# Four layers over eight batches: the quantiser in whole batches from an SBUF copy, merged on VectorE alone

## The chip, the core and the metric

One core of one Trainium2 chip. The metric is the time of one execution in microseconds (us), the median of several. The core has TensorE (PE) for matmuls, VectorE (DVE), ScalarE (ACT), GpSimd (POOL) and SyncE (SP), which here only issues DMAs. Each engine goes through a queue of its own in order; semaphores tie the queues together.

## The reference

x is 8 batches of 256 rows of 1024 numbers (fp32). Four layers, each added to its input:

```
x = x + x @ W0.T + 0.5 * (x @ A0[label]) @ B0.T                 # layer 0, one W0, rank 32
gi  = number of the 8 thresholds that |x| does not exceed
d, zp = delta[gi], zeropoint[gi]                                  # gi at most 7
x = x + (gi == 8 ? 0 : (clip(round(x / d) + zp, 0, 63) - zp) * d) # layer 1, the quantiser
x = x + x @ W2[adapter].T                                         # layer 2, one of 8 matrices a batch
x = x + (x @ B3[adapter].T) @ A3[adapter].T                       # layer 3, rank 16
```

`label` and `adapter` are read at run time, one for each batch.

## The kernel before

A batch lies transposed in SBUF: 128 partitions x 2048 columns, the column block k (256 columns, k = 0 to 7) holding features k*128 and on. The work is a pipeline over batches: in step s layer 0 and the quantiser work on batch s (stage a), layer 2 on batch s-1 (stage b), layer 3 on batch s-2 (stage c). `all_steps` writes steps 0, 1 and 6 to 9 out, steps 2 to 5 are a hardware loop of two steps a turn.

**TensorE.** `layer0(s, parity, half, tiles)` makes one output tile of 256 columns from 24 fp32r matmuls (W0 and x are each split into a high and a low part: hi*hi, hi*lo, lo*hi; L702) and one low-rank matmul (L711). Four tiles are a half, and a half fills two PSUM banks, `l0_ps[:, half]`. `low_rank0` (L723) makes the low-rank input of the next batch, `low_rank3` (L734) and `layer3` (L747) are layer 3, `layer2` (L783) is plain fp32, in four chunks q of two tiles, each in its own bank of two. `last_layer2` (L764) does the last batch with split operands. x_hi and x_lo have two buffers.

**The quantiser** works on a half, 1024 columns, straight from PSUM. For each of the 8 groups k ScalarE makes a candidate round(x/delta) (`candidate`, L408) and a mask in bf16 (`test`, L421) from the magnitude (L400); GpSimd rescales it for k = 1 to 7 (`rescale`, L309), VectorE for k = 0 (`scale`, L584); VectorE clips it (`clip`, L595 and L598) and merges it into x2 under the mask (`merge`, `copy_predicated`, L606), from the widest group inward; a last `copy_predicated` writes zeros (L647), and the layer-0 output is added from PSUM (L650). Three candidate and three mask buffers go round; a new candidate waits until the merge three back is done.

**Around it.** `drain_chunk` (L572) adds a layer-2 chunk to x2 into x3 on VectorE, `finish_chunk` (L562) a layer-3 chunk into one of two `result` buffers, which is stored. `chunks_after(k)` says between which merges they stand. `split_batch` makes x_hi on ScalarE (L356) and x_lo on VectorE (L478) for the next batch, `low_rank_hi`/`low_rank_lo` and `split_bx` (L534) split the low-rank inputs. The layer-3 matrix a3 is split on ScalarE (L447) and GpSimd (L335).

Of the kernel before, what the change touches and what calls it, by code (L numbers as in the profile page):

```python
# [6 lines left out]
ALU = mybir.AluOpType  # L7
ACT = mybir.ActivationFunctionType
F32 = mybir.dt.float32
F32R = mybir.dt.float32r  # L10
BF16 = mybir.dt.bfloat16
I16 = mybir.dt.int16
# [6 lines left out]
UW = BW // 2  # L19
CW = BW // 4  # L20
QUAD = 32
# [7 lines left out]
STEEP = 2.0 ** 40  # L29
BELOW_ONE = 1.0 - 2.0 ** -24  # L30
POOL_GROUPS = (1, 2, 3, 4, 5, 6, 7)


def build(nc, x, labels, adapters, thresholds, deltas, zeropoints, w0, a0, b0, w2, b3, a3, out):

    with ExitStack() as ctx:
# [13 lines left out]
        x_hi = sb("x_hi", [P, 2, BW], F32R)  # L60
        x_lo = sb("x_lo", [P, 2, BW], F32R)
# [4 lines left out]
        magnitude = sb("magnitude", [P, UW], F32)  # L66
        cand = sb("cand", [P, CANDS, UW], F32)
        mask = sb("mask", [P, MASKS, UW], BF16)
        x2 = sb("x2", [P, 2, BW], F32)
        x3 = sb("x3", [P, BW], F32)  # L70
        result = sb("result", [P, 2, CW], F32)
# [6 lines left out]
        zero = sb("zero", [P, 1], F32)  # L78
# [13 lines left out]
        l0_ps = ps("l0_ps", [P, 2, UW])  # L92
# [8 lines left out]
        x_loaded = sem("x_loaded")  # L101
# [9 lines left out]

        sp_waited = sem("sp_waited")
        dve_waited = sem("dve_waited")
        pool_waited = sem("pool_waited")
# [11 lines left out]
        low_split_done = sem("low_split_done")  # L126
        l0_done = sem("l0_done")
        mag_done = sem("mag_done")
        rounded = sem("rounded")
        masked = sem("masked")  # L130
        scaled_dve = sem("scaled_dve")
        scaled_pool = sem("scaled_pool")
        clipped = sem("clipped")
        merged = sem("merged")
        zeroed = sem("zeroed")
# [3 lines left out]
        last_x2_hi_done = sem("last_x2_hi_done")  # L139
        last_x2_split_done = sem("last_x2_split_done")  # L140
        last_w2_hi_done = sem("last_w2_hi_done")
        last_w2_split_pool = sem("last_w2_split_pool")
        last_w2_split_done = sem("last_w2_split_done")
# [8 lines left out]

        pool_share = len(POOL_GROUPS)
        dve_share = G - pool_share

        def all_steps(engine, step):


            step(0, 0, True, False, False)
            step(1, 1, True, True, False)  # L160
            with engine.Fori(1, B // 2 - 1) as pair:
                s = pair * 2
                step(s, 0, True, True, True)
                step(s + 1, 1, True, True, True)
            step(B - 2, 0, True, True, True)
            step(B - 1, 1, True, True, True)
            step(B, 0, False, True, True)
            step(B + 1, 1, False, False, True)

        def first(s):  # L170
            return isinstance(s, int) and s == 0

        def has_next(s):

            return not (isinstance(s, int) and s >= B - 1)

        def low_rank_at(s):

            if first(s):
                return 0, 6  # L180
            return (1, 4) if isinstance(s, int) and s == 1 else (1, 6)

        def l0_unit(s, half):


            if isinstance(s, int) and s == 1 and half == 1:
                return l2_ps[:, :, :].rearrange("p n w -> p (n w)")
            return l0_ps[:, half, :]

        def l2_bank(s, q):  # L190

            if isinstance(s, int) and s == 1:
                return l0_ps[:, 1, (q % 2) * CW:(q % 2 + 1) * CW]
            return l2_ps[:, q % 2, :]

        def l3_bank(s, q):

            if isinstance(s, int) and s >= B:
                return l0_ps[:, q // 2, (q % 2) * CW:(q % 2 + 1) * CW]
            return l3_ps[:, :]  # L200

        def result_chunk(s, parity, q):

            if isinstance(s, int) and s >= B:
                return x2[:, parity, q * CW:(q + 1) * CW]
            return result[:, q % 2, :]
# [4 lines left out]
        def _(sp):  # L211
            def load_x(n):
                sp.dma_start(x_raw[:, :], x[bass.ds(n, 1)].rearrange("b p w -> p (b w)")).then_inc(x_loaded, 16)

            def load_a0(n):
                label = sp.value_load(label_ids[0:1, bass.ds(n, 1)], min_val=0, max_val=a0.shape[0] - 1)
# [3 lines left out]
            for q in range(4):  # L220
                sp.sem_inc(out_stored[q], 1)

            load_x(0)
            sp.dma_start(w2_sb[:, 0, :], w0[0]).then_inc(w0_loaded[0], 16)
            sp.dma_start(label_ids[:, :], labels.rearrange("(a n) -> a n", a=1)).then_inc(ids_loaded, 16)
            sp.dma_start(adapter_ids[:, :], adapters.rearrange("(a n) -> a n", a=1)).then_inc(ids_loaded, 16)
            sp.dma_start(w2_sb[:, 1, :], w0[1]).then_inc(w0_loaded[1], 16)
# [4 lines left out]
            sp.dma_start(w2_sb[:, 2, :], w0[2]).then_inc(w0_loaded[2], 16)  # L232

# [3 lines left out]
            for o in range(3, T):  # L237
                sp.dma_start(w2_sb[:, o, :], w0[o]).then_inc(w0_loaded[o], 16)
            sp.wait_ge(x_split_done, 1)
            load_x(1)  # L240
            sp.wait_ge(a0_split_done, 1)
            load_a0(1)

            def step(s, parity, stage_a, stage_b, stage_c):

                if stage_a and not first(s) and has_next(s):

                    sp.wait_ge(x_split_done, s + 1)
                    sp.sem_inc(sp_waited, 1)
                    load_x(s + 1)  # L250
                    sp.wait_ge(a0_split_done, s + 1)
                    sp.sem_inc(sp_waited, 1)
                    load_a0(s + 1)
                if stage_b:

                    adapter = sp.value_load(adapter_ids[0:1, bass.ds(s - 1, 1)], min_val=0, max_val=b3.shape[0] - 1)
                    if stage_c:
                        sp.wait_ge(b3_done, s - 1)
                        sp.sem_inc(sp_waited, 1)
                        sp.wait_ge(a3_split_done, s - 1)  # L260
                        sp.sem_inc(sp_waited, 1)
                    else:
                        sp.wait_ge(gaps_zeroed, 2)
                    sp.dma_start(b3_raw[:, :, :].rearrange("p k r -> p (k r)"),
                                 b3[bass.ds(adapter, 1)].rearrange("l p w -> p (l w)")).then_inc(b3_loaded, 16)
                    for q in range(4):
                        sp.dma_start(a3_raw[q * QUAD:q * QUAD + R3, :],
                                     a3[bass.ds(adapter, 1)].rearrange("l r w -> r (l w)")).then_inc(a3_loaded, 16)
                if stage_a:
                    adapter = sp.value_load(adapter_ids[0:1, bass.ds(s, 1)], min_val=0, max_val=b3.shape[0] - 1)  # L270
                for q in range(4):
                    if stage_a:

                        if first(s):
                            sp.wait_ge(w0_split_done, 2 * q + 2)
# [580 lines left out]
```

## Time and profile before

| | before |
|---|---|
| median of 3 runs | 543.29 us (541.81 to 546.21) |
| profiled execution, its own time | 545.4 us |
| its span | 543.5 us |
| busy: PE, DVE, ACT, POOL | 483.3, 457.4, 341.3, 205.9 us |
| mean granted TensorE clock | 0.951 |

Busy time counts only work, not waits. In a row of the time order, the first two numbers are start and duration, both in us; in brackets stands the idle time ahead of it and what ended it. "x8" are instructions taken together; a fp32 matmul is recorded as two.

### The profile page before, as it was taken

The page shows a single profiled execution, that of the slowest core. Times are in us where ns is not written, and L with a number is a line of the kernel's source. Part 1 is how long each engine was busy: PE and PEld are TensorE (multiplying, and loading weights), DVE is VectorE, ACT ScalarE, POOL GpSimd, SP SyncE. Part 2 cuts the span into 40 slices and gives each one's busy share as a digit, 9 for nine tenths or more (in the row PEclk, how much of TensorE's full clock was granted, in tenths as well). Part 3 has the DMA queues.
Part 4 walks back from the last instruction along what each step waited for, and adds up shares of the span by engine and source line. Part 5 has one row for each costly group of instructions (what it writes and reads, how often), then busy time and mean ns, then how long its engine had stood idle before and what let it go on. Part 6 is the DMA issues. An engine that isn't in the chain of part 4 may idle for free.

```text
span 543.5 us, 8328 instructions
## 1 busy us (share of the span) xinstructions
PE 483.3 (89%) x3008; PEld 448.8 (83%) x3008; DVE 457.4 (84%) x423; ACT 341.3 (63%) x333; POOL 205.9 (38%) x139
## 2 busy tenths in 40 slices
PE   3886958889998999989999799989999799986895
PEld 3886957679887899869998699878998799975794
DVE  3778999999999939999599967999599996999962
ACT  4597778865786538763777619865487628676500
POOL 1035335355525425343244415245163434244410
PEclk9998987989999799989999799998999999999799
DMA  6863000324025150355105260252404430154022
GB/s 241 337 254 113 2 0 19 137 78 180 11 88 184 43 185 2 102 188 182 25 0 193 96 207 0 77 191 72 158 1 119 172 122 1 37 187 165 25 78 77
DMA packets 15507, 59.14 MB, mean 109 GB/s; under 512 B 2548, under 2 KB 4596, under 8 KB 10356
## 3 DMA queue, kind: packets, MB, share of 16 engines
q1 hardware_dynamic: 15476, 58.74, 31.2%
q8 instruction: 18, 0.29, 0.2%
q14 instruction: 13, 0.11, 0.1%
HBM read 50.34 MB, written 8.39 MB: 108 GB/s over the span
## 4 chain that ended last, share of the span: by engine, by line
DVE 42%; PE 35%; issue 12%; ACT 3%; DMA 2%; DVEq 2%; POOL 2%; SPq 1%; POOLq 0%; ACTq 0%
DVE cand L598 15%; PE l_ps L702 15%; DVE x L606 13%; PE l_ps L783 12%; PE l_ps L764 5%; DVE x_lo L478 3%; PE bx_ps L734 2%; DVE x L647 2%; DVE cand L584 2%; ACT cand L408 2%; POOL cand L309 2%; DVE result L562 1%; DMA w_sb<-w 1%; DVE w_lo L506 1%; PE l_ps L747 1%
## 5 line engine op out<-in xcount | busy, mean ns | idle before, releaser
L309 POOL TENSOR_SCALAR cand<-cand,delta 128x1024 f32<-128x1024 f32 x112 | 171.1, 1528 | 267.6 <-ACT cand L408 267.6
L783 PE MATMUL l_ps<-x,w_sb 128*128 128x256 f32 x896 | 208.4, 393 | 10.9 <-DVE x L650 8.3
L783 PEld LDWEIGHTS l_ps<-x,w_sb 128*128 128x128 f32 x896 | 176.0, 199 | 36.2 <-issue 11.4
L606 DVE COPY_PREDICATED x<-mask,cand 128x1024 f32<-128x1024 int16 x112 | 172.3, 1539 | 19.4 <-DVE cand L598 18.8
L408 ACT ACTIVATE cand<-l_ps,inv_delta 128x1024 f32<-128x1024 f32 x128 | 141.7, 1118 | 73.5 <-DVE x L606 48.7
L421 ACT ACTIVATE mask<-magnitude,thr_bias 128x1024 bf16<-128x1024 f32 x128 | 147.0, 1149 | 22.1 <-DVE x L606 21.7
L598 DVE TENSOR_SCALAR cand<-cand,lower,upper 128x1024 f32<-128x1024 f32 x112 | 131.6, 1175 | 7.2 <-POOL cand L309 7.2
L702 PE MATMUL l_ps<-x_hi,w_hi 128*128 128x256 f32 x512 | 75.7, 292 | 9.9 <-ACT w_hi L351 8.8
L702 PEld LDWEIGHTS l_ps<-x_hi,w_hi 128*128 128x128 f32 x512 | 68.3, 196 | 10.9 <-ACT w_hi L351 8.8
L702 PE MATMUL l_ps<-x_lo,w_hi 128*128 128x256 f32 x512 | 73.4, 287 | 0.0
L702 PE MATMUL l_ps<-x_hi,w_lo 128*128 128x256 f32 x512 | 72.5, 285 | 0.0
L702 PEld LDWEIGHTS l_ps<-x_lo,w_hi 128*128 128x128 f32 x512 | 67.6, 196 | 0.0
L702 PEld LDWEIGHTS l_ps<-x_hi,w_lo 128*128 128x128 f32 x512 | 66.8, 194 | 0.0
L400 ACT ACTIVATE magnitude<-l_ps 128x1024 f32<-128x1024 f32 x16 | 16.3, 1016 | 58.2 <-PE l_ps L711 56.2
L584 DVE TENSOR_SCALAR cand<-cand,delta 128x1024 f32<-128x1024 f32 x16 | 17.4, 1086 | 29.1 <-ACT cand L408 29.1
L734 PE MATMUL bx_ps<-x,b_wide 128*128 128x256 f32 x128 | 30.2, 388 | 5.4 <-DVE x L572 5.4
L734 PEld LDWEIGHTS bx_ps<-x,b_wide 128*128 128x128 f32 x128 | 24.2, 194 | 8.9 <-DVE x L572 5.8
L747 PE MATMUL l_ps<-bx_split,a_split 128*128 128x256 f32 x64 | 15.7, 344 | 17.7 <-DVE result L562 16.3
L335 POOL TENSOR_TENSOR a_split<-a_raw,a_split 64x1024 fp32r<-64x1024 f32 x8 | 21.6, 2704 | 25.6 <-ACT a_split L447 25.4
L572 DVE TENSOR_TENSOR x<-l_ps,x 128x512 f32<-128x512 f32 x32 | 21.8, 680 | 8.1 <-PE l_ps L764 7.9
L747 PEld LDWEIGHTS l_ps<-bx_split,a_split 128*128 128x128 f32 x64 | 10.9, 202 | 20.1 <-DVE result L562 17.7
L711 PE MATMUL l_ps<-low_split,b_split 128*128 128x256 f32 x64 | 18.3, 286 | 5.3 <-DVE low_split L490 5.3
(53 smaller groups left out, 317.3 us busy)
## 6 DMA issues: line engine op xcount, KB each, us to landing
w_sb<-w SPq DMA_DIRECT2D x32, 1024.0 KB, 5.3
x_raw<-x SPq DMA_DIRECT2D x8, 1024.0 KB, 7.5
out<-result SPq DMA_DIRECT2D x24, 256.0 KB, 5.4
w_sb<-w SPq DMA_DIRECT2D x8, 512.0 KB, 7.4
a_raw<-a SPq DMA_DIRECT2D x32, 64.0 KB, 3.7
out<-x SPq DMA_DIRECT2D x8, 256.0 KB, 2.2
a_raw<-a SPq DMA_DIRECT2D x8, 128.0 KB, 6.8
a_raw<-b SPq DMA_DIRECT2D x4, 128.0 KB, 2.6
```

Source lines behind the costliest of these rows:

```text
L309: pool.tensor_scalar(c, c, -ROUND, delta[:, k:k + 1], ALU.add, ALU.mult)\
L408: act.activation(cand[:, k % CANDS, :], src, ACT.Identity, bias=ROUND, scale=inv_delta[:, k:k + 1]).then_inc(rounded, 1)
L421: act.activation(mask[:, j % MASKS, :], magnitude[:, :], ACT.Relu, bias=thr_bias[:, j:j + 1], scale=-STEEP * BELOW_ONE).then_inc(masked, 1)
L572: dve.tensor_tensor(x3[:, cols], l2_bank(s, q), x2[:, 1 - parity, cols], ALU.add).then_inc(x3_done, 1)
L584: dve.tensor_scalar(c, c, -ROUND, delta[:, k:k + 1], ALU.add, ALU.mult)\
L598: dve.tensor_scalar(c, c, lower[:, k:k + 1], upper[:, k:k + 1], ALU.max, ALU.min)\
L606: dve.copy_predicated(y, mask[:, (k - 1) % MASKS, :].bitcast(I16), cand[:, k % CANDS, :])\
L702: nc.tensor.matmul(dst, w[:, o, k * P:(k + 1) * P], v[:, parity, k * S:(k + 1) * S], start=start, stop=False)
L734: last = nc.tensor.matmul(bx_ps[:, 0:S], b3_wide[:, k, :, :].rearrange("p q r -> p (q r)"), x3[:, k * S:(k + 1) * S], start=(k == 0), stop ...
L747: last = nc.tensor.matmul(l3_bank(s, q)[:, i * S:(i + 1) * S], a3_split[:, o * P:(o + 1) * P], bx_split[:, :], start=True, stop=True)
L764: last = nc.tensor.matmul(dst, w[:, o, k * P:(k + 1) * P], v[:, 1 - parity, k * S:(k + 1) * S], start=(v is x_hi and w is w0_hi and k == 0 ...
L783: last = nc.tensor.matmul(dst, w2_sb[:, o, k * P:(k + 1) * P], x2[:, 1 - parity, k * S:(k + 1) * S], start=(k == 0), stop=(k == T - 1))
```

## The change

- The hardware loop is gone, all is written out. TensorE has a list of its own: `AHEAD` says how many layer-0 tiles are done by the end of each step.
- ScalarE copies a layer-0 half to SBUF (`drain_l0`), into one of three x2 buffers. Magnitude, candidates and the last add work from there. For batches 1 to 6 a unit is the whole batch of 2048 columns, for batches 0 and 7 a half.
- The groups go innermost first (k = 7 - j). The first merge is a `scalar_tensor_tensor` that writes zero above the widest of its bounds, so that no separate zero pass is needed; seven `copy_predicated` follow, with masks of one byte. All eight rescales and the split of a3 are on VectorE, and GpSimd keeps only the copy of b3.
- x_hi and x_lo have one buffer, x comes in two halves, w0 tiles in the order 0, 2, 1, 3, 4, 6, 5, 7.
- Layer-3 results go into x3 in place and are stored from there. The last layer 2 is fp32 with the two halves of the sum apart, not split.

```diff
-                    pool.tensor_scalar(c, c, -ROUND, delta[:, k:k + 1], ALU.add, ALU.mult)\
-                        .then_inc(scaled_pool, 1)
...
-                dve.copy_predicated(y, mask[:, (G - 1) % MASKS, :].bitcast(I16), zero[:, :].to_broadcast([P, UW]))\
-                    .then_inc(zeroed, 1)
-                dve.wait_ge(zeroed, unit + 1)
-                dve.tensor_tensor(y, l0_unit(s, half), y, ALU.add).then_inc(x2_done, 1)
...
+UNITS = ((0, 0, HW), (0, HW, HW)) + tuple((b, 0, BW) for b in range(1, B - 1)) + ((B - 1, 0, HW), (B - 1, HW, HW))
...
+AHEAD = (20, 28, 32, 40, 48, 56, 64, 64)
...
         @block.scalar
...
+            def drain_l0(b, h):
+                act.wait_ge(l0_done, 2 * b + h + 1)
...
+                act.activation(x2[:, b % SLOTS, h * HW:(h + 1) * HW], l0_ps[:, h, :], ACT.Copy).then_inc(x0_done, 1)
...
+            def candidate(u, j):
...
+                if j == 0:
+                    act.wait_ge(x0_done, 2 * b + (first + n) // HW)
+                if c >= CANDS:
+                    act.wait_ge(merged, c - CANDS + 1)
+                act.activation(cand[:, c % CANDS, 0:n], x2_unit(u), ACT.Identity, bias=ROUND,
+                               scale=inv_delta[:, k:k + 1]).then_inc(rounded, 1)
...
+            def between(u, j):
...
+                elif s < B - 1:
+                    if j == 1:
+                        split_batch(s + 1)
+                    if j == 3:
+                        split_a3(s - 1)
+                    if j == 4:
+                        low_rank_hi(s + 1)
+                    if j == 6:
+                        split_bx(s - 1)
+                    if j == 7:
+                        drain_l0(s + 1, 0)
+                        drain_l0(s + 1, 1)
...
+            def quantise(u):
+                candidate(u, 0)
+                take_magnitude(u)
+                candidate(u, 1)
+                act.wait_ge(mag_done, u + 1)
+                for j in range(1, G):
+                    test(u, j)
+                    if j + 1 < G:
+                        candidate(u, j + 1)
+                    between(u, j)
...
         @block.vector
...
+            def merge(u, j):
...
+                if j == 0:
+                    dve.scalar_tensor_tensor(y, magnitude[:, 0:n], sorted_thr[:, G - 1:G], t, ALU.is_gt, ALU.mult)\
+                        .then_inc(merged, 1)
+                else:
...
+                    dve.copy_predicated(y, mask[:, m % MASKS, 0:n].bitcast(I8), t).then_inc(merged, 1)
...
+            def between(u, j):
...
+                elif s == 2:
+                    if j == 0:
+                        for q in range(4):
+                            finish(0, q)
...
+                elif s < B - 1:
+                    if j == 0:
+                        for q in range(4):
+                            if s == 3:
+                                finish(1, q)
+                    if j == 1:
+                        split_batch(s + 1)
+                        drain_l2(s - 1, 0)
+                    if j == 2:
+                        drain_l2(s - 1, 1)
+                    if j == 3:
+                        split_a3(s - 1)
+                        drain_l2(s - 1, 2)
+                    if j == 4:
+                        low_rank_lo(s + 1)
+                    if j == 5:
+                        drain_l2(s - 1, 3)
+                    if j == 6:
+                        split_bx(s - 1)
+                    if j == 7:
+                        for q in range(4):
+                            finish(s - 1, q)
...
+            def quantise(u):
+                scale(u, 0)
+                clip(u, 0)
+                for j in range(G):
+                    if j + 1 < G:
+                        scale(u, j + 1)
+                    merge(u, j)
+                    if j + 1 < G:
+                        clip(u, j + 1)
+                    between(u, j)
+                dve.wait_ge(merged, (u + 1) * G)
+                dve.tensor_tensor(x2_unit(u), x2_unit(u), quant[:, 0:UNITS[u][2]], ALU.add).then_inc(x2_done, 1)
...
         @block.tensor
...
+            def layer2(b, q):
+                pe.wait_ge(w2_loaded[q], (b + 1) * 16)
+                if q == 0:
+                    pe.wait_ge(x2_done, x2_count(b))
...
+                    if q > 1:
+                        pe.wait_ge(x3_done, b * 4 + q - 1)
...
+            def layer3(b, q):
...
+                if q == 3:
+                    pe.wait_ge(out_done, 4 * b + 1)
...
+            for n in range(AHEAD[0]):
+                tile0(n, False)
+            for s in range(1, B):
+                early = s > 2 and s + 1 < B
+                for q in range(4):
+                    if q == 3 and early:
+                        low_rank0(s + 1, s - 1)
+                    layer2(s - 1, q)
+                tiles = range(AHEAD[s - 1], AHEAD[s])
+                for i, n in enumerate(tiles):
+                    tile0(n, early)
+                    if i == 0:
+                        low_rank3(s - 1, min(n // T + 1, B))
+                    if i == 2:
+                        for q in range(3):
+                            layer3(s - 1, q)
+                    if i == min(4, len(tiles) - 1):
+                        layer3(s - 1, 3)
+                if not tiles:
+                    low_rank3(s - 1, B)
+                    for q in range(4):
+                        layer3(s - 1, q)
+            last_layer2(0)
+            last_layer2(1)
+            low_rank3(B - 1, B)
```

For batch 0 and 1, VectorE's `between` also holds the splits of the next batch (unit 0 at j = 4, unit 1 at j = 5, batch 1 at j = 7). In batch 7, `drain_l2(6, q)` stand in the first half at j = 3, 5, 7 and in the second at j = 1, `split_bx(6)` at j = 3 and `finish(6, q)` at j = 5 of the second.

## Rows read from the trace of the kernel before

**Rows 1.** The page: span, busy time, and the chain that ended last, by engine

```profile
span 543.5 us, 8328 instructions
...
PE 483.3 (89%) x3008; PEld 448.8 (83%) x3008; DVE 457.4 (84%) x423; ACT 341.3 (63%) x333; POOL 205.9 (38%) x139
...
DVE 42%; PE 35%; issue 12%; ACT 3%; DMA 2%; DVEq 2%; POOL 2%; SPq 1%; POOLq 0%; ACTq 0%
```

**Rows 2.** Windows of one batch each: length, busy times, clock, DMA

```profile
core 0: us, PE busy (x) PEld busy (x) DVE busy (x) ACT busy (x) POOL busy (x), PEclk, DMA share, GB/s
...
199.00:262.00 63.00, 60.39 (x373) 55.93 (x373) 53.97 (x49) 39.88 (x40) 24.36 (x16) 0.97 0.32 108
```

**Rows 3.** Order of time on TensorE, one batch: start, duration, line

```profile
190.19 1.12 PE L702 MATMUL l_ps<-x_hi,w_hi 128*128 128x256 f32 x8
...
199.20 3.62 PE L734 MATMUL bx_ps<-x,b_wide 128*128 128x256 f32 x16
202.46 1.30 PE L702 MATMUL l_ps<-x_hi,w_hi 128*128 128x256 f32 x8
...
214.64 0.40 PE L747 MATMUL l_ps<-bx_split,a_split 128*128 128x256 f32 x2
214.88 7.07 PE L783 MATMUL l_ps<-x,w_sb 128*128 128x256 f32 x32
221.60 0.59 PE L747 MATMUL l_ps<-bx_split,a_split 128*128 128x256 f32 x2
...
235.89 1.30 PE L723 MATMUL bx_ps<-x_hi,a_split 128*128 128x256 f32 x8
237.03 1.12 PE L723 MATMUL bx_ps<-x_lo,a_split 128*128 128x256 f32 x8
240.76 0.50 PE L747 MATMUL l_ps<-bx_split,a_split 128*128 128x256 f32 x2 [2.61 <-DVE result L562]
241.10 8.75 PE L783 MATMUL l_ps<-x,w_sb 128*128 128x256 f32 x32
...
277.13 0.40 PE L747 MATMUL l_ps<-bx_split,a_split 128*128 128x256 f32 x2
```

**Rows 4.** Order of time on TensorE, the first layer 2

```profile
83.68 15.97 PE L783 MATMUL l_ps<-x,w_sb 128*128 128x256 f32 x64 [8.34 <-DVE x L650]
```

**Rows 5.** Order of time on VectorE, inside one quantiser

```profile
149.92 0.79 DVE L598 TENSOR_SCALAR cand<-cand,lower,upper 128x1024 f32<-128x1024 f32 x1
150.96 1.32 DVE L606 COPY_PREDICATED x<-mask,cand 128x1024 f32<-128x1024 int16 x1 [0.25 <-DVE cand L598]
152.17 1.61 DVE L598 TENSOR_SCALAR cand<-cand,lower,upper 128x1024 f32<-128x1024 f32 x1
...
168.21 0.81 DVE L595 TENSOR_SCALAR x<-cand,lower,upper 128x1024 f32<-128x1024 f32 x1
168.94 0.81 DVE L598 TENSOR_SCALAR cand<-cand,lower,upper 128x1024 f32<-128x1024 f32 x1
```

**Rows 6.** Groups of instructions: count, busy us, mean ns, idle before them

```profile
L598 DVE TENSOR_SCALAR cand<-cand,lower,upper 128x1024 f32<-128x1024 f32 x112 | 131.6, 1175 | 7.2 <-POOL cand L309 7.2
...
L572 DVE TENSOR_TENSOR x<-l_ps,x 128x512 f32<-128x512 f32 x32 | 21.8, 680 | 8.1 <-PE l_ps L764 7.9
L650 DVE TENSOR_TENSOR x<-l_ps,x 128x1024 f32<-128x1024 f32 x16 | 19.6, 1224 | 0.6
...
L478 DVE TENSOR_TENSOR x_lo<-x_raw,x_hi 128x2048 fp32r<-128x2048 f32 x8 | 18.3, 2287 | 0.3 <-ACT x_hi L356 0.3
...
L356 ACT ACTIVATE x_hi<-x_raw 128x2048 fp32r<-128x2048 f32 x8 | 15.2, 1902 | 3.7 <-DMA x_raw<-x 3.7
...
L534 DVE TENSOR_TENSOR bx_split<-bx_ps,bx_split 32x256 fp32r<-32x256 f32 x16 | 6.8, 424 | 3.6 <-ACT bx_split L385 3.1
```

**Rows 7.** Order of time on TensorE, its first matmuls

```profile
8.85 2.07 PE L702 MATMUL l_ps<-x_hi,w_hi 128*128 128x256 f32 x8 [8.85 <-ACT w_hi L351]
```

**Rows 8.** The chain that ended last, in order of time, start of the quantiser

```profile
28.00 1.02 ACT magnitude L400
```

**Rows 9.** The chain that ended last, in order of time, its end

```profile
532.78 3.47 PE bx_ps L734 x16
538.17 1.29 DVE x L562 x2
```

More of the change, by code:

```diff
@@ L151, in build, with units_of, x2_count, x2_unit @@
         out_done = sem("out_done")
[L153 to L193, printed above, removed]
-            return l2_ps[:, q % 2, :]
[L196 to L206, printed above, removed]
+        def units_of(b):
+            return [u for u, unit in enumerate(UNITS) if unit[0] == b]
+        def x2_count(b):
+            return units_of(b)[-1] + 1
+        def x2_unit(u):
+            b, first, n = UNITS[u]
+            return x2[:, b % SLOTS, first:first + n]
+        def l2_bank(b, q):
+            if b == B - 1:
+                return l0_ps[:, q // 2, (q % 2) * CW:(q % 2 + 1) * CW]
+            return l2_ps[:, q % 2, :]
+        def l3_bank(q):
+            return l3_ps[:, :] if q in (0, 3) else l2_ps[:, q - 1, :]
         block = ctx.enter_context(nc.Block())
@@ L470, in _ @@
+            split_w0(0)
+            split_x(0, 1)
+            split_a0(0)
+            split_w0(1)
+            act.wait_ge(b0_loaded, 4 * 16)
+            act.activation(b0_split[:, :], a3_raw[:, :], ACT.Copy, scale=0.5).then_inc(b0_hi_done, 1)
+            low_rank_hi(0)
+            for n in range(2, T):
+                split_w0(n)
+            drain_l0(0, 0)
             act.wait_ge(param_step, 6)
-            all_steps(act, step)
+            for u in range(len(UNITS)):
+                quantise(u)
@@ new lines, in scale, with clip @@
+            def scale(u, j):
+                n = UNITS[u][2]
+                c = u * G + j
+                k = G - 1 - j
+                t = cand[:, c % CANDS, 0:n]
+                dve.wait_ge(rounded, c + 1)
+                dve.tensor_scalar(t, t, -ROUND, delta[:, k:k + 1], ALU.add, ALU.mult).then_inc(scaled, 1)
+            def clip(u, j):
+                n = UNITS[u][2]
+                c = u * G + j
+                k = G - 1 - j
+                t = cand[:, c % CANDS, 0:n]
+                dve.wait_ge(scaled, c + 1)
+                dve.tensor_scalar(t, t, lower[:, k:k + 1], upper[:, k:k + 1], ALU.max, ALU.min).then_inc(clipped, 1)
@@ L538, in _ @@
+            low_rank_lo(0)
+            for n in range(2, T):
+                if n + 1 < T:
+                    add_diag(n + 1)
+                split_w0(n)
             dve.wait_ge(params_loaded, 3 * 16)
@@ L721, in low_rank0 @@
+            def low_rank0(b, after):
+                pe.wait_ge(x_split_done, 2 * b + 2)
+                pe.wait_ge(a0_split_done, b + 1)
+                if after > 0:
+                    pe.wait_ge(bx_split_done, 2 * after)
                 for v in (x_hi, x_lo):
@@ new lines, in last_layer2 @@
+            def last_layer2(half):
+                b = B - 1
+                if half == 0:
+                    pe.wait_ge(x0_done, 2 * B)
+                pe.wait_ge(x2_done, x2_count(b) - 1 + half)
+                for q in range(4):
+                    if half == 0:
+                        pe.wait_ge(w2_loaded[q], (b + 1) * 16)
+                    for i in range(2):
+                        o = 2 * q + i
+                        for k in range(half * HALF, (half + 1) * HALF):
+                            last = nc.tensor.matmul(l2_bank(b, q)[:, i * S:(i + 1) * S],
+                                                    w2_sb[:, o, k * P:(k + 1) * P],
+                                                    x2[:, b % SLOTS, k * S:(k + 1) * S],
+                                                    start=(i == 0 and k == 0), stop=(i == 1 and k == T - 1))
+                    if half == 1:
+                        last.then_inc(l2_done, 1)
@@ L819 @@
+            last_layer2(0)
+            last_layer2(1)
+            low_rank3(B - 1, B)
+            for q in range(4):
+                layer3(B - 1, q)
 def kernel(x, itok_B_0_2, condB_thresholds, condB_deltas, condB_zeropoints, itok_B_3_7, L0_cond_W,
```

829 lines of the change are left out of this document (373 added, 456 removed).

## The prediction

> **What bounds the kernel now.** I read the page first, then the windows, the groups, and the order of time on VectorE and TensorE. VectorE (84%) and TensorE (89%) are both nearly full, and the chain that ended last changes between them [rows 1]. One loop step (one batch) takes 63 us, with TensorE busy for 60 of it and VectorE for 54 [rows 2]. So the question is not which engine has more work, but whether the new order lets both run at the same time.
>
> What TensorE needs for a batch at the full clock: three layer-0 tiles take 199.20 - 190.19 = 9.01 us, 3.0 a tile, so 24.0 for eight; `low_rank3` 3.3 (202.46 - 199.20); a layer-2 chunk 221.60 - 214.88 = 6.7, four 26.9; `low_rank0` 2.1 to 2.3; four layer-3 chunks about 0.4 each, 1.7 [rows 3]. Sum 58. The rest of the 63 is waiting and its echo: after 2.61 us of idle the same chunk took 8.75 us and not 7.07 [rows 3], and after 8.34 us of idle two chunks took 15.97 where two in a row need 13.4 [rows 4]. I charge 2.3 us for each wait of three microseconds or more; the rows give 1.7 to 2.8.
>
> **VectorE's new work.** A clip of 1024 columns takes 0.79 when GpSimd does nothing, 1.61 when a GpSimd rescale runs beside it [rows 5], 1.175 in the mean over 112 [rows 6]. The change takes the rescale off GpSimd, so clips fall to 0.8, but adds eight rescales a batch to VectorE. None of 2048 columns is in the trace. Lower bound 0.79 (width is free), upper bound 1.58 (twice the instruction); I take 1.33, because the two-input subtraction grows from 1.22 at 1024 to 2.29 at 2048 [rows 6], 0.16 fixed and 1.06 for each 1024, and the scalar pass streams in half of that. `copy_predicated` of 1024 takes 1.32 undisturbed [rows 5]; at 2048 I take 2.4, between 1.32 and 2.64. The new mask has one byte and not two; no row shows what that does, and I keep 1.32 (twice as quick) as its lower end. Consecutive independent passes start 0.08 before the one ahead has ended (168.21 + 0.81 against 168.94) [rows 5].
>
> The Trainium skill (VectorE: DVE Perf Modes, "The perf-mode tier table") gives 1227 ns for an fp32 `tensor_scalar` of 2048 in SBUF. By it the seven such passes ahead of the first drain would take 0.7 us less in a batch, and the period worked out below would be 65.8 and not 66.5. The same page ("The TRN2 errata") speaks against the SBUF copy: ScalarE's fixed part is 224 cycles from SBUF and 172 from PSUM, by which 17 passes cost it 0.7 us a batch more; no row here compares one form from both.
>
> By these, one `quantise` of 2048 costs 16 scalar passes x 1.24 + first merge (`scalar_tensor_tensor`, as a two-input pass) 2.2 + 7 x 2.3 + last add 2.4 = 40.5 us. Beside it stand the splits of x (2.3), a0 (0.3), low (0.3), a3 (1.1, new here, before on GpSimd), bx (0.8), four drains and four finishes at 0.6 (4.8) [rows 6]: 9.6. Together 50.1, a gain of 4 on the busy 54 [rows 2]. ScalarE: 2048 columns take 1.90 [rows 6], so 7 tests, 8 candidates and a magnitude take 30, with all else 40. Neither is the bound; TensorE's 58 would be, if nothing stopped it.
>
> **What stops it.** Before, a half's magnitude and candidates are taken from the layer-0 bank as soon as four tiles are done. After, `candidate(u, 0)` waits for both halves, thus for the last tile of TensorE's step. Call that end E. In the same step `layer2` of the batch before starts at E, fills its two banks by E + 13.5, and chunk 2 waits for `drain_l2(s-1, 0)`, which stands in VectorE's queue behind j = 1. Steady steps (s = 4, 5, 6), counted from E:
> - ScalarE drains the second half (1.1), candidate 0 (1.9): VectorE starts at E + 3.0.
> - scale 0, clip 0: 5.8. Candidate 1 is behind the magnitude, 3.8 after candidate 0: scale 1 ends at 8.1. Merge 0, clip 1: 11.5. Scale 2, merge 1, clip 2: 16.3. Split of the next x and a0: 18.9. Drain 0: 19.6.
> - TensorE has stood still for 19.6 - 13.5 = 6.1 us and then runs slowly (2.3). Left to do: chunk 2, `low_rank0`, chunk 3 (15.6), eight tiles (24), `low_rank3` (3.3), layer 3 (1.7) = 44.6.
> - Period 19.6 + 44.6 + 2.3 = 66.5 us against 63.2 before. VectorE's end in it is at about E + 60, since `finish(s-1, 3)` waits for the layer-3 chunk behind tile 4: it has slack, and its gain isn't used.
>
> **The start.** In halves and with w0 tile 0 earlier, TensorE may start 1 us sooner than at 8.85 [rows 7]. Parameters still hold the quantiser to 28 us [rows 8]. x_hi and x_lo have one buffer now, so `split_batch` waits until all tiles of the batch ahead are done; TensorE then waits from 37.5 to 45, and batch 0's x2 is ready at 85, against 83.7 before (the layer-2 matmul that it releases) [rows 4]. TensorE by then works ahead: tile 19 ends at 92, layer 2 of batch 0 at 119, tile 23 at 137, tile 24 with its low rank at 142.5. There `layer3(0, 3)` waits for `finish(0, 0)`, which stands behind j = 0 of the next unit: its candidate 0 is ready at 142, clip 1 ends at 150.4, finish at 151: 8.5 us idle. Step 1 ends at 163. Step 2 (27 + 12 tiles + 3.3 + 1.3) ends its last tile at 207, and `layer3(1, 3)` waits for `finish(1, 0)`, which needs candidates that need that tile: 1.1 + 1.9, then to clip 1 (8.5), 0.6: 12.1 us idle, TensorE goes on at 219. Step 3 ends at 280. Before, the same layer-0 batch ended at 277 (the layer-3 chunk behind it starts at 277.13, 62.5 after that of 214.64) [rows 3]: the start costs 3 us, since the gain of the first batches is eaten by the two waits.
>
> **Steps 4 to 6:** 280 + 3 x 66.5 = 480. Moved stores (`finish` into x3, no `result` ring) wait on SP in a row behind loads that are due a step later; I cost them at nothing. If that cover were gone, a w2 chunk late by its 5 us would stop TensorE by that much once a step.
>
> **The end.** Units 8 and 9 have 1024 columns (22.6 us each, 0.8 a scalar pass and 1.32 a merge). Unit 8 starts at 482.7 (both halves are drained before its candidate), ends with its three drains and a3 at 509; unit 9 reaches j = 5 at 527.5. `finish(6, 0)` at 528 releases `layer3(6, 3)`, behind which TensorE's queue holds `last_layer2(0)`: its input was ready at 509, but it starts at 528.6. 13.5 + 2.3, then the second half 13.5: 558. Last drain and the end of `low_rank3` 559.8. Before, the last `low_rank3` ended at 536.25 (532.78 + 3.47), 7.3 ahead of the end of the span [rows 9]. So 567.
>
> I take 565 for the span, some rounding of waits downward, 567 for its own time by the 1.9 us around the span of before (545.4 against 543.5). The median of before is 2.1 below its profiled execution, thus 565 as the forecast, +4%.
>
> **Rivals.**
> 1. *Milder:* TensorE's echo is small (1.7) and the wide passes are quicker (merge 1.33 by the byte mask). The first drain comes 3 us sooner, period 62.9; three steps give back 11, the end 5. 545 to 556, middle 549. For it: the low ends of the bounds; against it: five of the seven passes of the chain are scalar ones with a narrow bound.
> 2. *Faster:* the width is nearly free (scalar pass 0.8, merge 1.33). From VectorE's start to drain 0 it is then 16.6 - 6.7 = 9.9 and drain 0 falls to E + 12.9, ahead of the 13.5 at which TensorE needs it. From there on TensorE isn't stopped: period 58.2 x 3 gives back 25, the two waits of steps 1 and 2 some 12, the end 10: 518. It decides at a saving of 6.1 us ahead of drain 0. Against it: the subtraction nearly doubles with width [rows 6].
> 3. *The change doesn't do what it says:* clips aren't slowed by GpSimd but by what is beside them (ScalarE, DMA), and stay at a mean of 1.18 for 1024, 2.2 for 2048. Then a batch costs VectorE 50.1 + 16 x 0.9 = 65, each fixed term above grows, and the period is 72: 590. Against it: 0.79 and 1.61 in the same stage [rows 5].
> 4. *Heavier:* the forecast, with a late load, with a mask pass on ScalarE that is slower to write one byte, or with the straight code not there in time: 580.
>
> **Chances and range.** The forecast 0.50 (556 to 575), milder 0.18 (of it 0.10 within 1%), faster 0.18, the third 0.05, heavier 0.09. A difference under 1% is about what a measurement of this kernel can't tell from none. Faster by over 1% 0.18, within 1% 0.10, slower 0.72. The range leaves out faster and the third: 545 to 582.
>
> **What would show it.** Right: in each step from the fourth on, layer-2 matmuls with some 6 us idle before the third chunk, released by VectorE's drain; 8 and 12 us idle ahead of single layer-3 chunks in steps 1 and 2; scalar passes near 1.33, merges near 2.4; VectorE under 80% busy; granted clock below 0.95. Wrong: layer-2 chunks in an unbroken row with a period under 60, or VectorE without idle time. The weakest number is the 16.6 us from VectorE's start to the first drain, as it is paid in every step.

## The result and the profile after

The changed kernel takes 576.01 us in the median (575.32 to 578.92), the one before 544.12 beside it: ratio 1.060 (95% interval 1.054 to 1.066), slower. The profiled execution has a span of 574.2 us.

The page of the kernel after: busy times, groups (count, busy us, mean ns, idle ahead), and the chain that ended last by engine.

```profile
PE 490.4 (85%) x2944; PEld 451.7 (79%) x2944; DVE 432.7 (75%) x393; ACT 312.8 (54%) x235; POOL 17.1 (3%) x16
...
PE 56%; DVE 23%; issue 9%; ACT 8%; DMA 2%; SPq 1%; DVEq 0%; ACTq 0%
...
L304 ACT ACTIVATE x<-l_ps 128x1024 f32<-128x1024 f32 x16 | 16.3, 1019 | 100.5 <-PE l_ps L685 100.5
```

VectorE is busy for 25 us less than before [rows 1] (the prediction's 4 us a batch would be 32), and still the time is longer: its own work isn't what decides. ScalarE's copy from PSUM (L304) waits 100 us in all for layer 0. TensorE's share of the chain has risen from 35% to 56%.

The groups with the shapes apart give the prices that no row of before had:

```profile
L523 DVE COPY_PREDICATED quant<-mask,cand 128x2048 f32<-128x2048 int8 x42 | 105.0, 2500 | 0.2
...
L505 DVE TENSOR_SCALAR cand<-cand,lower,upper 128x2048 f32<-128x2048 f32 x48 | 65.5, 1365 | 0.2
L497 DVE TENSOR_SCALAR cand<-cand,delta 128x2048 f32<-128x2048 f32 x48 | 61.7, 1286 | 51.5 <-ACT cand L334 51.1
L523 DVE COPY_PREDICATED quant<-mask,cand 128x1024 f32<-128x1024 int8 x28 | 37.2, 1328 | 0.1
```

Taken 1.33 for a scalar pass, measured 1.29 and 1.37; taken 2.4 for a merge, measured 2.5. At 1024 columns the merge with a one-byte mask takes 1.33, as the undisturbed one with two bytes (1.32) [rows 5]: the mask's width gives nothing there.

Order of time on TensorE, one steady step (s = 6), L730 being layer 2, L758 `low_rank3`, L770 layer 3:

```profile
416.60 13.98 PE L730 MATMUL l_ps<-x,w_sb 128*128 128x256 f32 x64
436.55 10.00 PE L730 MATMUL l_ps<-x,w_sb 128*128 128x256 f32 x32 [5.97 <-DVE x L484]
446.20 1.30 PE L696 MATMUL bx_ps<-x_hi,a_split 128*128 128x256 f32 x8
...
448.30 7.07 PE L730 MATMUL l_ps<-x,w_sb 128*128 128x256 f32 x32
...
458.20 3.62 PE L758 MATMUL bx_ps<-x,b_wide 128*128 128x256 f32 x16
...
483.61 13.98 PE L730 MATMUL l_ps<-x,w_sb 128*128 128x256 f32 x64
```

The step lasts 483.61 - 416.60 = 67.0 us (the two ahead of it 66.8 and 65.9). Two chunks run, then 5.97 us are idle until VectorE's drain (L484), and the third chunk then takes 10.00 where 7.07 is normal. That is TensorE's granted clock: 0.50, the lower of its two levels (1.2 and 2.4 GHz), from 436.60 to 440.00, and 1.00 again from 443.00 on. VectorE in the step ahead (it begins at E = 350.69):

```profile
353.98 1.29 DVE L497 TENSOR_SCALAR cand<-cand,delta 128x2048 f32<-128x2048 f32 x1 [9.20 <-ACT cand L334]
355.30 1.35 DVE L505 TENSOR_SCALAR cand<-cand,lower,upper 128x2048 f32<-128x2048 f32 x1
357.68 1.28 DVE L497 TENSOR_SCALAR cand<-cand,delta 128x2048 f32<-128x2048 f32 x1 [1.03 <-ACT cand L334]
...
367.18 2.37 DVE L447 TENSOR_TENSOR x_lo<-x_raw,x_hi 128x1024 fp32r<-128x1024 f32 x2
369.45 0.43 DVE L452 TENSOR_TENSOR a_split<-a_raw,a_split 128x256 fp32r<-128x256 f32 x1
369.79 0.70 DVE L484 TENSOR_TENSOR x<-l_ps,x 128x512 f32<-128x512 f32 x1
```

It idles for 9.20 us, starts at E + 3.3 (predicted 3.0) and ends the first drain at E + 19.8 (predicted 19.6). Both engines idle in every step, each once for the other.

The single layer-3 chunks of steps 1 and 2 and the end, on TensorE:

```profile
151.97 0.80 PE L770 MATMUL l_ps<-bx_split,a_split 128*128 128x256 f32 x2 [8.29 <-DVE x L489]
...
159.08 0.80 PE L685 MATMUL l_ps<-low_split,b_split 128*128 128x256 f32 x2 [2.13 <-DVE low_split L463]
...
223.25 0.80 PE L770 MATMUL l_ps<-bx_split,a_split 128*128 128x256 f32 x2 [12.41 <-DVE x L489]
...
532.30 0.79 PE L770 MATMUL l_ps<-bx_split,a_split 128*128 128x256 f32 x2 [4.34 <-DVE x L489]
532.89 30.27 PE L745 MATMUL l_ps<-x,w_sb 128*128 128x256 f32 x128
```

### The profile page after: what moved, and what is told of

Read it like the earlier page. It is cut to its first block, busy times and chain, and to the rows that moved or that the text cites. A ratio compares the mean times of both kernels' runs of the same rounds, so it can differ in the third digit from the quotient of the medians.

```text
span 574.2 us, 7145 instructions
## 1 busy us (share of the span) xinstructions
PE 490.4 (85%) x2944; PEld 451.7 (79%) x2944; DVE 432.7 (75%) x393; ACT 312.8 (54%) x235; POOL 17.1 (3%) x16
## 4 chain that ended last, share of the span: by engine, by line
PE 56%; DVE 23%; issue 9%; ACT 8%; DMA 2%; SPq 1%; DVEq 0%; ACTq 0%
PE l_ps L673 24%; PE l_ps L730 19%; DVE quant L523 6%; PE l_ps L745 5%; DVE cand L497 4%; PE bx_ps L758 4%; ACT cand L334 4%; DVE quant L517 3%; ACT magnitude L324 2%; DVE cand L505 2%; PE bx_ps L696 2%; DVE x_lo L447 1%; DVE x L484 1%; DMA w_sb<-w 1%; DVE w_lo L441 1%
## 5 line engine op out<-in xcount | busy, mean ns | idle before, releaser
L730 PE MATMUL l_ps<-x,w_sb 128*128 128x256 f32 x896 | 206.4, 393 | 21.2 <-DVE x L484 20.8
L730 PEld LDWEIGHTS l_ps<-x,w_sb 128*128 128x128 f32 x896 | 176.3, 198 | 48.4 <-issue 23.0
L523 DVE COPY_PREDICATED quant<-mask,cand 128x2048 f32<-128x2048 int8 (+1 forms) x70 | 142.2, 2031 | 0.4
L334 ACT ACTIVATE cand<-x,inv_delta 128x2048 f32<-128x2048 f32 (+1 forms) x80 | 132.2, 1652 | 12.8 <-DVE quant L523 8.9
L497 DVE TENSOR_SCALAR cand<-cand,delta 128x2048 f32<-128x2048 f32 (+1 forms) x80 | 85.8, 1073 | 66.5 <-ACT cand L334 66.1
L344 ACT ACTIVATE mask<-magnitude,thr_bias 128x2048 fp8e5<-128x2048 f32 (+1 forms) x70 | 115.4, 1648 | 0.0
L673 PE MATMUL l_ps<-x_hi,w_hi 128*128 128x256 f32 x512 | 88.3, 297 | 19.9 <-DVE x_lo L447 19.9
L505 DVE TENSOR_SCALAR cand<-cand,lower,upper 128x2048 f32<-128x2048 f32 (+1 forms) x80 | 91.7, 1147 | 0.4
L673 PEld LDWEIGHTS l_ps<-x_hi,w_hi 128*128 128x128 f32 x512 | 74.8, 200 | 21.0 <-issue 12.1
L304 ACT ACTIVATE x<-l_ps 128x1024 f32<-128x1024 f32 x16 | 16.3, 1019 | 100.5 <-PE l_ps L685 100.5
L770 PE MATMUL l_ps<-bx_split,a_split 128*128 128x256 f32 x64 | 12.4, 321 | 32.9 <-DVE x L489 25.3
L484 DVE TENSOR_TENSOR x<-l_ps,x 128x512 f32<-128x512 f32 x32 | 22.2, 694 | 23.0 <-PE l_ps L745 19.6
L770 PEld LDWEIGHTS l_ps<-bx_split,a_split 128*128 128x128 f32 x64 | 9.9, 215 | 34.6 <-DVE x L489 26.3
L489 DVE TENSOR_TENSOR x<-l_ps,x 128x512 f32<-128x512 f32 x32 | 20.3, 685 | 19.4 <-PE l_ps L770 19.2
L758 PE MATMUL bx_ps<-x,b_wide 128*128 128x256 f32 x128 | 29.6, 381 | 1.5 <-DVE x L484 1.5
L745 PE MATMUL l_ps<-x,w_sb 128*128 128x256 f32 x128 | 30.3, 402 | 0.0
L745 PEld LDWEIGHTS l_ps<-x,w_sb 128*128 128x128 f32 x128 | 26.1, 205 | 4.0
```

The costliest lines, as they stand in the source:

```text
L334: act.activation(cand[:, c % CANDS, 0:n], x2_unit(u), ACT.Identity, bias=ROUND, scale=inv_delta[:, k:k + 1]).then_inc(rounded, 1)
L344: act.activation(mask[:, m % MASKS, 0:n], magnitude[:, 0:n], ACT.Relu, bias=thr_bias[:, k:k + 1], scale=STEEP, saturate=False).then_inc(ma ...
L484: dve.tensor_tensor(x3[:, cols], l2_bank(b, q), x2[:, b % SLOTS, cols], ALU.add).then_inc(x3_done, 1)
L489: dve.tensor_tensor(x3[:, cols], l3_bank(q), x3[:, cols], ALU.add).then_inc(out_done, 1)
L497: dve.tensor_scalar(t, t, -ROUND, delta[:, k:k + 1], ALU.add, ALU.mult).then_inc(scaled, 1)
L505: dve.tensor_scalar(t, t, lower[:, k:k + 1], upper[:, k:k + 1], ALU.max, ALU.min).then_inc(clipped, 1)
```

## The experiments

Theory: the queues' order sets the time (which drain, finish or split stands behind which pass). Rivals: VectorE simply has too much work, or whole-batch units are slow in themselves. All but e8 start from the changed kernel, 1.060 times before; each ratio below is against the kernel before on the same chip.

**e1: one drain moved.**

```diff
+                    if j == 0:
+                        drain_l2(s - 1, 0)
                     if j == 1:
                         split_batch(s + 1)
-                        drain_l2(s - 1, 0)
```

> The changed kernel with one move on VectorE: in batches 3 to 6 the first layer-2 drain stands behind j = 0 and not behind j = 1 and the split. Queue-order theory: the 6 us idle before the third layer-2 chunk goes (steps 4 to 6), but low_rank3 then waits for the fourth drain, which still stands behind j = 5, 43 us into the step; the period falls by 1 us at most, 573 to 576 us. Prediction as written (the first drain alone sets the period): 8 us less in each of three steps, 552. Rival, VectorE simply has too much work: no change, and no idle time moved, 576.

Measured 582.5 us, ratio 1.070 (1.064 to 1.077): no gain, and 6 us above every number expected. The execution profiled was the fastest, 578.2. TensorE in one step of e1:

```profile
352.58 20.89 PE L731 MATMUL l_ps<-x,w_sb 128*128 128x256 f32 x96
378.03 8.83 PE L731 MATMUL l_ps<-x,w_sb 128*128 128x256 f32 x32 [2.66 <-DVE x L484]
390.03 0.39 PE L686 MATMUL l_ps<-low_split,b_split 128*128 128x256 f32 x1 [0.29 <-DVE low_split L463]
390.25 2.75 PE L759 MATMUL bx_ps<-x,b_wide 128*128 128x256 f32 x12
395.65 1.59 PE L759 MATMUL bx_ps<-x,b_wide 128*128 128x256 f32 x4 [2.64 <-DVE x L484]
```

Three chunks now run unbroken (x96). The 6 us come back as 2.66 ahead of the fourth chunk, waiting for the second drain, and 2.64 inside `low_rank3`, waiting for the fourth. In the steps beside it the low-rank split is a third such wait (2.03 and 2.07), and the three steps last 66.0, 67.5 and 66.1 us, as before the move. Step 3, which had no wait above 0.5 us in its layer 2 and `low_rank3`, now has 2.65 in `low_rank3` and lasts 64.8 us instead of 59.4. The first drain was only the first of several waits in one chain.

**e2: all drains forward, `split_bx` and the low-rank split behind j = 4.**

```diff
+                    if j == 0:
+                        drain_l2(s - 1, 0)
                     if j == 1:
+                        drain_l2(s - 1, 1)
                         split_batch(s + 1)
-                        drain_l2(s - 1, 0)
                     if j == 2:
-                        drain_l2(s - 1, 1)
+                        drain_l2(s - 1, 2)
                     if j == 3:
                         split_a3(s - 1)
-                        drain_l2(s - 1, 2)
+                        drain_l2(s - 1, 3)
                     if j == 4:
                         low_rank_lo(s + 1)
+                        split_bx(s - 1)
...
+                    if j == 6:
+                        for q in range(3):
+                            finish(s - 1, q)
                     if j == 7:
-                        for q in range(4):
-                            finish(s - 1, q)
+                        finish(s - 1, 3)
```

> The changed kernel, batches 3 to 6: drains behind j = 0, 1, 2, 3, split_bx behind j = 4, finishes 0 to 2 behind j = 6. Same instructions, other order. Queue-order theory: TensorE runs nearly unbroken, period 59 to 60 instead of 66, some 20 us less in all, 555. Rival, VectorE's added work sets the period: 574 to 577.

Measured 594.8 us, ratio 1.092 (1.085 to 1.099): slower still, and above both numbers. TensorE and VectorE of e2:

```profile
401.78 0.58 PE L685 MATMUL l_ps<-low_split,b_split 128*128 128x256 f32 x1 [5.34 <-DVE low_split L462]
402.16 5.30 PE L758 MATMUL bx_ps<-x,b_wide 128*128 128x256 f32 x16
```

```profile
401.29 0.43 DVE L462 TENSOR_TENSOR low_split<-bx_ps,low_split 32x256 fp32r<-32x256 f32 x1
407.91 0.88 DVE L475 TENSOR_TENSOR bx_split<-bx_ps,bx_split 32x256 fp32r<-32x256 f32 x2 [6.19 <-ACT bx_split L316]
411.69 1.29 DVE L496 TENSOR_SCALAR cand<-cand,delta 128x2048 f32<-128x2048 f32 x1 [2.90 <-ACT cand L334]
```

TensorE reached the first tile's close before VectorE's low-rank split (5.34 us idle), so `low_rank3` came late, and `split_bx`, moved ahead of its input, held VectorE for 6.19 us and the candidates behind it on ScalarE for another 2.90. On TensorE itself the steps show two waits, 5.3 us for the low-rank split and 2.2 for a finish, and last 69.3 to 70.5 us. The same work and no slower pass (clips of 2048 columns 1.34, merges 2.49), 19 us more: order alone can cost that much.

**e5: the same with these two placed by when their inputs are there.**

```diff
                     if j == 3:
+                        low_rank_lo(s + 1)
                         split_a3(s - 1)
...
-                    if j == 4:
-                        low_rank_lo(s + 1)
...
+                    if j == 5:
+                        split_bx(s - 1)
```

> As e2_all_drains_early, but low_rank_lo behind j = 3 ahead of the split of a3, and split_bx behind j = 5 (in e2 the one came 5.3 us too late for the close of the first tile and the other stopped VectorE and ScalarE for 6 us). Same instructions as the changed kernel. Queue-order theory: no wait of TensorE is longer than 2 us in steps 4 to 6, period 60 instead of 66.5, 556 us. Rival, VectorE's added work sets the period whatever the order: 574 or, as e2, above.

Measured 558.9 us, ratio 1.030 (1.025 to 1.036), 17 us under the changed kernel. TensorE of e5:

```profile
284.57 20.89 PE L731 MATMUL l_ps<-x,w_sb 128*128 128x256 f32 x96
307.21 7.07 PE L731 MATMUL l_ps<-x,w_sb 128*128 128x256 f32 x32
328.67 0.98 PE L771 MATMUL l_ps<-bx_split,a_split 128*128 128x256 f32 x6 [1.96 <-DVE bx_split L476]
...
344.73 20.89 PE L731 MATMUL l_ps<-x,w_sb 128*128 128x256 f32 x96
```

344.73 - 284.57 = 60.2 us a step, with whole-batch units, every rescale on VectorE, and one wait of 1.96. The next step is the same; the third waits 2.01 too but lasts 61.7, as the granted clock falls behind its wait (0.69 over the 3 us that follow, against 1.00 in the two steps ahead).

**e3: finishes of batches 0 and 1 at the end of the unit ahead.**

```diff
                     if j == 7:
                         split_bx(0)
+                        for q in range(3):
+                            finish(0, q)
                         split_batch(3)
...
                     if j == 0:
-                        for q in range(4):
-                            finish(0, q)
+                        finish(0, 3)
```

The same for batch 1.

> The changed kernel with finish(0, 0..2) and finish(1, 0..2) moved from j = 0 of the next unit to the end of the unit ahead, where VectorE idles. Queue-order theory: the 8.3 and 12.4 us waits before the single layer-3 chunks go, but low_rank_lo(3) behind j = 1 stops TensorE for most of the first, and step 3 now shows the 6 us idle of steps 4 to 6; net 9 to 14 us less, 564. As predicted blind, both waits fully given back: 552. Rival, total VectorE work: 576.

Measured 567.9 us, ratio 1.043 (1.036 to 1.050). TensorE of e3:

```profile
157.72 0.79 PE L687 MATMUL l_ps<-low_split,b_split 128*128 128x256 f32 x2 [10.28 <-DVE low_split L463]
...
231.04 9.36 PE L732 MATMUL l_ps<-x,w_sb 128*128 128x256 f32 x32 [5.57 <-DVE x L484]
```

Both waits are gone, but the low-rank split of batch 3 stops TensorE for 10.28 us where 8.29 + 2.13 stood, and step 3 shows the 5.57 us that the long wait had covered. 21 us of waits removed gave back 8, a little less than the 9 to 14 expected.

**e4: the end.** `last_layer2(0)` directly behind `low_rank3(6)`; the finishes of batch 6 and `split_a3(7)` behind the last unit; `layer3(6, 3)` behind the first chunk of `last_layer2(1)`.

```diff
-                    for q in range(4):
-                        layer3(s - 1, q)
-            last_layer2(0)
-            last_layer2(1)
+            last_layer2(0, range(4))
+            for q in range(3):
+                layer3(B - 2, q)
+            last_layer2(1, range(1))
+            layer3(B - 2, 3)
+            last_layer2(1, range(1, 4))
```

> The changed kernel with another order at its end: last_layer2(0) directly behind low_rank3(6), the finishes of batch 6 behind the last unit, layer3(6, 3) inside last_layer2(1). Queue-order theory: last_layer2(0) runs while VectorE quantises, the end comes 11 us sooner, 565. Rival: VectorE's quantiser of the last batch sets the end and the moved finishes only shift it, 574 to 577.

Measured 566.0 us, ratio 1.039 (1.032 to 1.047), 10 us under the changed kernel. TensorE of e4:

```profile
520.89 13.98 PE L743 MATMUL l_ps<-x,w_sb 128*128 128x256 f32 x64
...
537.67 5.41 PE L743 MATMUL l_ps<-x,w_sb 128*128 128x256 f32 x16 [2.10 <-DVE x L613]
```

The first half of the last layer 2 now runs while VectorE still quantises, and only 2.10 us are left ahead of the second half, where the changed kernel had 6.17 and 4.34 ahead of the first.

**e6, e7 and e9: the same two added passes in three places.** A clip is done three times instead of once.

```diff
+                for i in range(2):
+                    if count[0]:
+                        dve.wait_ge(again, count[0])
+                    dve.tensor_scalar(t, t, lower[:, k:k + 1], upper[:, k:k + 1], ALU.max, ALU.min).then_inc(again, 1)
+                    count[0] += 1
+                dve.wait_ge(again, count[0])
```

> The changed kernel with one clip done three times instead of once (the result is the same) behind j = 1 in batches 3 to 6, ahead of the split and the first drain. Two passes of 1.3 and a handover are 2.75 us. Queue-order theory: this place is on the path, each step is 2.75 longer, 10 to 11 us in all, 586. Rival, only total work of VectorE counts: the same as e7_two_clips_late.

> The same two passes more, but behind j = 6, after the drains and splits. Queue-order theory: hidden, VectorE idles 9 to 12 us at the end of each step and the finishes are 4.4 us early, 576. Rival, total work of VectorE counts: 10 us more, 586, as e6_two_clips_early.

> As e7_two_clips_late, but the two added clips stand behind split_bx in j = 6 and not ahead of it (in e7 TensorE waited up to 1.8 us for split_bx, which I had overlooked: its slack is 0.9). Queue-order theory: hidden, as the finish that TensorE needs is 4.4 us early: 575 to 577. Rival, total work of VectorE counts: 581 to 584, as e6 and e7.

Measured: ahead of the first drain 583.5 us (ratio 1.073, 1.069 to 1.078); ahead of `split_bx` 581.4 (1.069, 1.064 to 1.074); behind `split_bx` 575.5 (1.058, 1.051 to 1.066), the changed kernel's own time. e7 missed: TensorE waited 0.76, 0.60 and 1.77 us for `split_bx` in steps 4 to 6. I had put the slack at 4.4 from the finishes; that of `split_bx` was 0.9 to 1.9. In e6 the idle time ahead of the third chunk rose from 5.97 to 8.87, the period by 2.7. Eight passes of 1.37 us (11 us in all) cost 8, 5 or 0 us by their place; VectorE's total work is refuted as the cause.

**e8: one part of the change alone, in the kernel before.**

```diff
-POOL_GROUPS = (1, 2, 3, 4, 5, 6, 7)
+POOL_GROUPS = (7,)
```

> The kernel before with rescales 1 to 6 of each half on VectorE too, only that of group 7 on GpSimd: one part of the change alone. It adds 12 passes of 0.72 us a batch to VectorE, 8.6, and takes away most of the time that clips and merges lose beside GpSimd (9 us a batch by the means over the undisturbed values). Port theory: clips fall to a median of 0.80 and a mean under 0.9, the time stays within 6 us of the kernel before, 544. Rival (third of the prediction), the clips are slow for another reason: mean stays near 1.18 and the time grows by 8 times 8 us, 600.

Measured 525.9 us, ratio 0.968 (0.963 to 0.972): 18 us faster, more than I allowed for. Groups of e8:

```profile
L606 DVE COPY_PREDICATED x<-mask,cand 128x1024 f32<-128x1024 int16 x112 | 160.5, 1433 | 7.0 <-DVE cand L598 6.3 <-ACT mask L421 0.5
L598 DVE TENSOR_SCALAR cand<-cand,lower,upper 128x1024 f32<-128x1024 f32 x112 | 104.4, 932 | 0.0
L584 DVE TENSOR_SCALAR cand<-cand,delta 128x1024 f32<-128x1024 f32 x112 | 86.7, 782 | 16.3 <-ACT cand L408 16.1
```

Clips fell from 1.175 to 0.932 (not quite under 0.9), merges from 1.539 to 1.433; 96 more rescales cost 69 us and VectorE's busy time rose by only 13 (457 to 470). TensorE's wait for VectorE's layer-3 results fell from 16.3 to 7.1 us, and its mean granted clock rose from 0.951 to 0.971: in the kernel before, the layer-2 chunk behind that wait took from step to step 9.85, 8.75, 9.66, 8.43 and 7.07 us, in e8 always 7.07. These two, 9.2 and 8.4 us, make up most of the 19.8 between the two traces. Why VectorE's results come sooner isn't tried apart: its passes are quicker, and a handover to GpSimd and back is gone from each of the moved rescales.

**e10: the same part undone in the changed kernel.**

```diff
+                    pool.wait_ge(rounded, c + 1)
+                    pool.tensor_scalar(t, t, -ROUND, delta[:, k:k + 1], ALU.add, ALU.mult).then_inc(scaled_pool, 1)
```

> The changed kernel with the rescales j = 1 to 7 of every unit on GpSimd again: undoes one part alone. Port theory: clips of 2048 rise from 1.36 to over 2 in the mean, merges too, and the first drain comes later although VectorE has 7 passes less: 585 to 600. Rival, the 7 passes (9 us a batch) are a burden that GpSimd could carry: the first drain comes 2.5 us sooner, 570 or less.

Measured 589.1 us, ratio 1.085 (1.077 to 1.092), 13 us more. Clips of 2048 take 1.71 (less than the 2 expected), merges 3.00 instead of 2.50, and the third layer-2 chunk waits 8.00 us instead of 5.97. Moving the rescales was a gain in both kernels.

**e11 and e12: all orders together,** the low-rank split of batch 3 behind j = 0, and in e12 layer 3 one tile later.

```diff
-                    if i == 2:
+                    if i == (3 if s > 2 else 2):
...
-                    if i == min(4, len(tiles) - 1):
+                    if i == min(5 if s > 2 else 4, len(tiles) - 1):
```

> All reorderings of the changed kernel together (e5, e3, e4), and the low-rank split of batch 3 moved ahead to j = 0, which e3 showed as a wait of 10.3 us. Queue-order theory: 17 (e5) + 8 (e3) + 10 (e4) + 6 for step 3, where e3's own wait reappears and e5 removes it + 6 for the low-rank split = 47 us less than the changed kernel, 529. If the gains overlap: 540 or more.

> As e11_all_orders, but from step 3 on the layer-3 chunks stand one tile later in TensorE's queue (0 to 2 behind tile 3, 3 behind tile 5), as e11 shows TensorE waiting 1.7 to 2.1 us for split_bx in each of four steps. Queue-order theory: these waits go and nothing else comes late, 8 us less than e11, 523 to 525, thus about level with e8 and some 4% under the kernel before. Rival: VectorE, now 59 us a step with its finishes, sets the period by itself, and the wait only moves: 529 to 532.

e11: 531.7 us, ratio 0.976 (0.968 to 0.983), between its two numbers: 44 of the 47 us came. e12: 518.9 us, ratio 0.961 (0.957 to 0.966), the fastest of all. TensorE of e12:

```profile
380.76 20.89 PE L731 MATMUL l_ps<-x,w_sb 128*128 128x256 f32 x96
403.39 7.07 PE L731 MATMUL l_ps<-x,w_sb 128*128 128x256 f32 x32
438.70 13.98 PE L731 MATMUL l_ps<-x,w_sb 128*128 128x256 f32 x64
```

438.70 - 380.76 = 57.9 us: the 58 that TensorE needs at the full clock (granted clock 1.00 in this step and the two ahead). No wait of TensorE is left in a steady step. Against e11 the times differ by 13 us, the two ratios by only 8, since the kernel before was faster too beside e12 (540.6 against 544.6). The traces show the step itself: four steps took 245.0 us in e11 and 231.8 in e12. In e11 they lasted 60.0 to 61.7, so a wait of 1.7 to 2.1 us, with the slower matmuls that followed some of them, cost 2 to 3.8.

e8's one line and the whole change in its best order thus end close to each other: 0.968 (0.963 to 0.972) and 0.961 (0.957 to 0.966). No run shows e8 with its own order improved, nor the changed kernel with half units in every batch, so what the whole-batch units are worth by themselves stays open.

## Why the prediction was right, and where it was not

- **Direction and mechanism:** right. The period (66.5 predicted; 66.8, 65.9, 67.0 measured), the 6.1 us idle (5.96 to 5.97), 8.5 (8.29) and 12.1 (12.41) came as worked out, and so did the slow third chunk (2.3 charged; 2.7, 1.8 and 2.9 measured). Rivals 2 (width nearly free) and 3 (clips slow anyway) are refuted by the passes of 1.29 to 1.37. So is rival 1: a merge of 2048 took 2.50, not 1.33. Of rival 4 nothing is seen: ScalarE's mask passes took 1.99 like its candidates, and TensorE's only wait in steps 4 to 6 is the one for the drain.
- **567 by the sum, 565 forecast, 576 measured.** The sum was of the span, which measured 574.2. It is 7 us too small in the start and the end; taking another 2 off for rounding had no ground in a row. The time lies inside the stated range, but 1 us above the 556 to 575 in which the forecast itself was to fall.
- **The start, 3.9 us too small.** Step 3 ended at 283.9 and not at 280, and all of it was there when step 1 ended, at 166.9 and not at 163. 1.0 had come by 151.97, where the first wait ended. The term left out is `low_rank_lo(3)`, behind j = 1: 2.13 us idle, and matmuls at a granted clock of 0.50 behind it.
- **The end, 3.5 us too small.** From E of step 6 to the end 90.6 us, predicted 87.1. The wait for `finish(6, 0)` isn't the reason: it started 48.0 us after E, as predicted, and was later only by what the start had lost. The last layer 2 began 0.7 later than worked out and took 0.8 more. The sum then has the end of `low_rank3` 1.8 us behind the last chunk, but its 16 matmuls alone need 3.5 [rows 9]: this is the term that is mis-sized, by 1.7. The rest is 0.3 in the tail.
- **Smaller slips of the sum.** Two chunks of 15.97 are set against 13.4, a distance from start to start; two unbroken ones have a duration of 13.98, so that wait cost 2.0 and not 2.6. The period of 65.8 counts seven scalar passes ahead of drain 0. There are six, and two of them end before VectorE waits for a candidate anyway (1.03 us at 357.68), so the shorter pass would give 0.4 and not 0.7; at 1.29 and 1.37 the measured ones are longer than it in any case. ScalarE reads 9 passes a batch from SBUF instead of PSUM, not 17; its magnitude of 1024 columns took 1.044 us after and 1.016 before.
- **"The first drain sets the period" was incomplete.** It held for the changed kernel, where no other wait appeared. e1 moved that drain and nothing was won: the second and the fourth drain and the low-rank split stood up to 2.7 us behind it. That they were in time in the changed kernel wasn't worked out, and here the period was right with some luck. For the same reason rival 2 is wrong in its turning point: 6.1 us ahead of drain 0 alone would not have been enough.
- **VectorE's gain "isn't used":** right for the changed kernel. But I weighed the move of the rescales as 4 us of busy time a batch and never asked what it would give in the old order. e8 shows 18 us there.
- **Where the expected gain went:** into an order in which the quantiser of a whole batch starts behind TensorE's last tile, while TensorE's next chunks wait for drains behind that quantiser's first passes. e5 leaves units, widths and engines as they are and wins 17; e12 shows that the whole loss, and more, was order.

## What to carry to other kernels

When two engines each wait for the other once in a step, write down for every shared result when it is made and when it is wanted, counted from the step's start, and move all that are late together: moving one only shows the next. A result moved ahead of its own input stops everything behind it in the queue; e2 had one such and one that was late, and lost 19 us by the two together. And try each part of a large change alone: one part here was worth 3% (e8) and was buried under an order that cost 10% (1.060 against 0.961).

## What the runs showed of the hardware that was not expected

- A one-byte mask makes `copy_predicated` neither quicker nor slower at 1024 columns: 1.33 us, against 1.32 undisturbed with two bytes [rows 5]. At 2048 columns, where only the one-byte mask was run, it takes 2.50.
- GpSimd's passes slow `copy_predicated` too, which reads two tensors in SBUF, mask and candidate: 2.50 without, 3.00 with rescales on GpSimd (e10). The Trainium skill (SBUF — State Buffer, "Who interferes with whom") says that a VectorE instruction with two SBUF inputs contends with a GpSimd one that reads SBUF; the runs agree. The one copy left on GpSimd (b3) took 0.67 us before and 1.82 in the changed kernel, but 1.09 to 1.13 in e2, e8, e10 and e12; what sets it isn't shown.
- TensorE after 5.96 to 5.98 us of idle: the same chunk took 8.56 to 10.09 us over the steps of the changed kernel and e7, against 7.07 unbroken, at the same idle time; the mean granted clock in it was 0.83 and 0.70. Shorter waits differ as much: in the kernel before, the chunk took 8.75 behind 2.61 us of idle and 7.07, at a clock of 1.00, behind 2.86.
